# Routing's end in a top-2 mixture of experts: padding rows stored earlier by two queues, the tile table in wide operations, two weights before the first rows, 103 tiles for 104

## The chip, the cores and the metric

The kernel runs on one core of one Trainium2 chip. The metric is the device time of one execution in microseconds (us). Its engines are TensorE (PE, with weight loads shown as PEld), VectorE (DVE), ScalarE (ACT), GpSimd (POOL) and SyncE (SP). A q behind an engine's name (SPq, ACTq, POOLq) is its instruction queue, which also issues DMA transfers. L12 is line 12 of the kernel.

## What is computed

The reference, cut to its frame:

```python
h = tok_ref(...)                       # a state-space kernel, 8 x 256 tokens
h = concatenate([h, txt], axis=1)      # 8 x 768 tokens of width 256
h = h + attn_ref(layernorm(h))         # 16 heads, 4 key/value heads
h = h + ffn_ref(layernorm(h))

def ffn_ref(x, Wr, br, W1, b1, W2, b2):          # E = 8 experts, H = 256
    logits = xf @ Wr + br                        # 6144 tokens
    topk_w, topk_idx = top_k(logits, 2)
    topk_w = softmax(topk_w)
    gate = sum(one_hot(topk_idx, E) * topk_w[..., None], axis=1)
    h = relu(einsum('th,ehf->etf', xf, W1) + b1) # f = 512
    y = einsum('etf,efh->eth', h, W2) + b2
    return einsum('te,eth->th', gate, y)
```

All arithmetic is float32. The kernel computes an expert only for the tokens that chose it.

## The kernel before

There are three stages: the state-space kernel, attention, and a last stage that has routing and the experts in one block, so that each engine's program runs from the one into the other without a barrier. Both belong to the change.

**Routing** (`route`) goes over 8 batches of 768 tokens, six tiles of 128 rows each. TensorE projects attention's output (L983), VectorE adds the residual into `h1` and normalizes into `xn` (L1106), TensorE transposes (L991) and computes the logits (L999), and VectorE picks the two best experts (`choose`) and the slot of every chosen row (`place`). Slots lie in DRAM in `xs_d`, with one region of `STRIDE` = 6144 + 128 rows for each expert; `run` holds the next free slot of every region. GpSimd scatters the rows of a tile to the slots, in 12 indirect DMAs a batch (L966). A batch's turn, logits and placing run beside the next batch's projection; those of the last batch stand in `drain` and have nothing beside them.

Behind the last batch come three steps. First, VectorE computes the tables of the expert tiles (`tile_table`): for each of `NT` = 104 tiles the expert (`exp_i`), the first row in `xs_d` (`src_i`) and the value that gates compare with (`held_by`), by a chain of small operations on 128x8 and 128x1, and then a loop over seven experts of three operations on 128x104. Its first instruction also copies `run` into `tail_i`, the slot behind the last row of each region; its last one raises `table_ready`. Secondly, ScalarE's queue, which waits for `table_ready` in its `drain`, stores 128 padding rows (`pads`) at each of the eight tails (L1068, L1069), so that a tile that is partly filled reads rows which add nothing. Thirdly, SyncE's queue, which waits for `table_ready` at the end of its part of `route`, issues the loads of the first four tiles' weights W1 (L1265, L1266), waits until pads, `h1` and scattered rows have landed (`landed`, L1271), and then loads the rows of the first four tiles (L1261, L1262).

**Experts** (`experts`) runs over the `NT` tiles of 128 rows with a ring of four buffers. For tile j TensorE transposes the rows of tile j+1 (L1293), multiplies tile j by W1 in 16 matmuls (`up`, L1303), and tile j-1 by W2 in 8 (`down`, L1310). ScalarE copies the transposed rows and applies the relu (L1333, L1341). VectorE adds the biases and multiplies by the gate (L1374 to L1394). GpSimd adds the 128 rows of the result into DRAM by an indirect DMA (L1360), for even tiles into the output and for odd ones into `acc2_d`. SyncE loads rows and W1 of tile j+4 as soon as the buffers of tile j are free. Four tiles are written out, a hardware loop runs the middle, and four more are written out (`loop`). At the end GpSimd waits for the adds of both accumulators and adds `acc2_d` into the output in eight DMAs (L1367).

Rows fill at most 96 + 7 tiles, since 12288 rows are 96 x 128 and each of the eight regions rounds up. A tile behind the last filled one repeats it with a gate of zero.

Of the kernel before, what the change touches and what calls it, by code (L numbers as in the profile page):

```python
# [17 lines left out]
P = 128  # L18
NB, SEQ, D = 8, 768, 256
# [4 lines left out]
TT = SEQ // P  # L24
IT = IMG // P
KC = D // P
TOK = NB * SEQ
# [4 lines left out]
NIT = NB * KV  # L32
STRIDE = TOK + P
SLOTS = NE * STRIDE
NT = TOK * TOPK // P + NE
DX = D + 8

F32 = mybir.dt.float32
# [832 lines left out]
def route(nc, block, sb, PS, sem, io, ident, img_d, oT_d, xs_d, acc_d, oT, oT_in, wo_in, h1, run, base, exp_i, src_i, tail_i, held_by, wo, wr, br, weights, weights_in, table_ready):  # L871
# [32 lines left out]
    rstd_ready, run_ready, xn_free = sem("r_rstd_ready"), sem("r_run_ready"), sem("r_xn_free")  # L904
    tr_done, xT_ready, lg_done = sem("r_tr_done"), sem("r_xT_ready"), sem("r_lg_done")
    mask_ready, count_done, gap_ready, ex_ready, idx_ready = (sem(f"r_{n}") for n in ("mask_ready", "count_done", "gap_ready", "ex_ready", "idx_ready"))
    table_dve, zeroed = sem("r_table_dve"), sem("r_zeroed")
    h_stored = sem("r_h_stored")
    norm_dve, pick_dve, place_dve = sem("r_norm_dve"), sem("r_pick_dve"), sem("r_place_dve")
    scattered = [sem(f"r_scattered{q}") for q in range(2)]  # L910
    TURN_AT, LOGITS_AT, COUNTS_AT = 1, 2, 3
# [14 lines left out]
    @block.sync  # L926
    def _(sp):
        sp.nop().then_inc(oT_free, 3)

        assert NE == NB  # L930
        for b in range(NB):
            if b + 1 < NB:
                sp.wait_ge(oT_free, b * TT + 3)
                load_rows(sp, oT, oT_d, oT_in, b + 1, (b + 1) % 2)
            sp.dma_start(b1[:, b], io["b1"][b].rearrange("(c p) -> p c", p=P), allow_slow_non_contiguous=True).then_inc(weights_in, 16)
            sp.dma_start(w2[:, b], io["W2"][b].rearrange("(c p) f -> p c f", p=P)).then_inc(weights_in, 16)
            sp.dma_start(b2[:, b], io["b2"][b].unsqueeze(0).to_broadcast([P, D])).then_inc(weights_in, 16)
        sp.wait_ge(weights_in, 3 * NE * 16)
        sp.wait_ge(table_ready, 1)

    @block.gpsimd
# [86 lines left out]
    @block.scalar  # L1028
    def _(act):
        def root(b):  # L1030
            act.wait_ge(var_ready, b + 1)
            act.activation(sd[:], ve[:], ACT.Sqrt).then_inc(sd_ready, 1)

        def turned(b):
            for n in range(3):
                act.wait_ge(tr_done, b * 3 + n + 1)
                act.activation(xT[:].rearrange("p c s -> p (c s)")[:, 512 * n:512 * n + 512], XT[:, n], ACT.Copy).then_inc(xT_ready, 1)

        def exp_gap(b):
            act.wait_ge(gap_ready, b + 1)  # L1040
            act.activation(ex[:], dl[:], ACT.Exp).then_inc(ex_ready, 1)

        def store(b):
            act.wait_ge(h1_ready, b * TT + (TT + 3))
            act.dma_start(acc_d[bass.ds(b * SEQ, SEQ), :].rearrange("(t p) d -> p t d", p=P), h1[:, b]).then_inc(h_stored, 16)

        def load(b, q):
            act.dma_start(h1[:, b, 0:IT, :], img_d[b].rearrange("(t p) d -> p t d", p=P)).then_inc(h_in[q], 16)
            act.dma_start(h1[:, b, IT:TT, :], io["txt"][b].rearrange("(t p) d -> p t d", p=P)).then_inc(h_in[q], 16)

        def iteration(b, q):
            if not first(b):
                turned(b - 1)
                if not isinstance(b, int):
                    load(b + 1, 1 - q)
                exp_gap(b - 1)
            root(b)
            store(b)

        load(0, 0)  # L1060
        load(1, 1)

        def drain():
            turned(NB - 1)
            exp_gap(NB - 1)
            act.wait_ge(table_ready, 1)
            for x in range(NE):
                row = act.value_load(tail_i[0:1, x:x + 1], min_val=x * STRIDE, max_val=x * STRIDE + TOK)  # L1068
                act.dma_start(xs_d[bass.ds(row, P), :], pads[:]).then_inc(zeroed, 16)  # L1069

        loop(iteration, drain, act)

    @block.vector
    def _(v):
# [88 lines left out]
        def drain():  # L1163
            choose(NB - 1)
            place(NB - 1, 1)
            tile_table(v, sb, table_dve, run, base, tile_no, exp_i, src_i, tail_i, held_by).then_inc(table_ready, 1)

        v.nop().then_inc(h1_ready, 3)
        v.nop().then_inc(mask_ready, 1)
# [3 lines left out]
        v.wait_ge(run_ready, 1)  # L1173
        loop(iteration, drain, v)

    return [(zeroed, 16 * NE), (h_stored, 16 * NB)] + [(scattered[q], NB // 2 * TT * TOPK * 16) for q in range(2)]


def tile_table(v, sb, dve, run, base, j, exp_i, src_i, tail_i, held_by):

    n, cnt, end = sb("t_n", [P, NE]), sb("t_cnt", [P, NE]), sb("t_end", [P, NE])
    ni = sb("t_ni", [P, NE], I32)
    last = sb("t_last", [P, 1])
    jr, e, start, ind = (sb(f"t_{x}", [P, NT]) for x in ("jr", "e", "start", "ind"))
    k = Tally(v, dve)
    link, mark = k.link, k.mark  # L1190
    mark(v.tensor_copy(tail_i[:], run[:]))
    mark(v.memset(e[:], 0.0))
    mark(v.memset(start[:], 0.0))
    link(v.tensor_tensor(n[:], run[:], base[:], ALU.subtract))
    link(v.tensor_scalar(ni[:], n[:], float(P - 1), None, ALU.add))
    link(v.tensor_scalar(ni[:], ni[:], 7, None, ALU.arith_shift_right))
    link(v.tensor_copy(cnt[:], ni[:]))
    link(v.tensor_copy(end[:, 0:1], cnt[:, 0:1]))
    for x in range(1, NE):
        link(v.tensor_tensor(end[:, x:x + 1], end[:, x - 1:x], cnt[:, x:x + 1], ALU.add))  # L1200
    link(v.tensor_scalar(last[:], end[:, NE - 1:NE], -1.0, None, ALU.add))
    link(v.tensor_scalar(jr[:], j[:], last[:], None, ALU.min))
    for x in range(NE - 1):
        link(v.tensor_scalar(ind[:], jr[:], end[:, x:x + 1], None, ALU.is_ge))  # L1204
        mark(v.tensor_tensor(e[:], e[:], ind[:], ALU.add))  # L1205
        link(v.scalar_tensor_tensor(out=start[:], in0=ind[:], scalar=cnt[:, x:x + 1], in1=start[:], op0=ALU.mult, op1=ALU.add))
    link(v.tensor_tensor(start[:], jr[:], start[:], ALU.subtract))
    link(v.tensor_scalar(start[:], start[:], float(P), None, ALU.mult))
    mark(v.tensor_copy(exp_i[:], e[:]))
    link(v.tensor_scalar(ind[:], j[:], last[:], None, ALU.is_gt))  # L1210
    mark(v.scalar_tensor_tensor(out=held_by[:], in0=ind[:], scalar=-2.0 * NE, in1=e[:], op0=ALU.mult, op1=ALU.add))
    return v.scalar_tensor_tensor(out=src_i[:], in0=e[:], scalar=float(STRIDE), in1=start[:], op0=ALU.mult, op1=ALU.add)


def experts(nc, block, sb, PS, sem, io, ident, xs_d, acc_d, acc2_d, exp_i, src_i, held_by, weights, landed, table_ready):
# [26 lines left out]
    def loop(eng, tile):  # L1242

        for n in range(RING):
            tile(n, n)
        with eng.Fori(1, NT // RING - 1) as k:
            for n in range(RING):
                tile(k * RING + n, n)
        for n in range(RING):
            tile(NT - RING + n, n)  # L1250

    def more(j, ahead):
        return not (isinstance(j, int) and j + ahead >= NT)
# [4 lines left out]
    @block.sync  # L1258
    def _(sp):
        def load(j, n):  # L1260
            row = sp.value_load(at(src_i, j), min_val=0, max_val=SLOTS - P)  # L1261
            sp.dma_start(x[:, n, :], xs_d[bass.ds(row, P), :]).then_inc(x_in[n], 16)  # L1262

        def load_w1(j, n):
            ex = sp.value_load(at(exp_i, j), min_val=0, max_val=NE - 1)  # L1265
            sp.dma_start(w1[:, n], io["W1"][bass.ds(ex, 1)].rearrange("o (c p) f -> p (o c) f", p=P)).then_inc(w1_in[n], 16)  # L1266

        for n in range(RING):
            load_w1(n, n)
        for s, value in landed:  # L1270
            sp.wait_ge(s, value)  # L1271
        for n in range(RING):
            load(n, n)

        def tile(j, n):
            if more(j, RING):
                hold(sp, xt_done, j + 1)
                hold(sp, gate_ready, j + 1)
                load(j + RING, n)
                hold(sp, h_done, j + 1)  # L1280
                load_w1(j + RING, n)

        loop(sp, tile)
        sp.wait_ge(summed, 16 * NB)

    @block.tensor
    def _(pe):
# [35 lines left out]

        turn_x(0, 0)
        loop(pe, tile)
        down(NT - 1, 1, expert(NT - 1))

    @block.scalar
    def _(act):
# [23 lines left out]
    @block.gpsimd  # L1353
    def _(pool):
        def tile(j, n):
            hold(pool, y_ready, j + 1)
            q = n % 2
            if not (isinstance(j, int) and j < 2):
                hold(pool, added[q], (j >> 1) * 16)
            pool.indirect_dma_start(out=(acc_d, acc2_d)[q], out_offset=bass.IndirectOffsetOnAxis(ap=row_i[:, n:n + 1], axis=0),  # L1360
                                    in_=y[:, n, :], in_offset=None, compute_op=ALU.add, bounds_check=TOK - 1, oob_is_err=False).then_inc(added[q], 16)

        loop(pool, tile)
        for q in range(2):
            hold(pool, added[q], NT // 2 * 16)
        for b in range(NB):
            pool.dma_start(rows(acc_d, b), rows(acc2_d, b), accum_op=ALU.add, max_dma_last_dim=6144).then_inc(summed, 16)  # L1367

    @block.vector
    def _(v):  # L1370
# [30 lines left out]

        hold(v, table_ready, 1)
        loop(v, tile)
        bias_y(NT - 1, RING - 1)


def program(nc, x, txt, log_dt, inv_A_real, A_imag, B_ri, Wq, Wk, Wv, Wo, Wr, br, W1, b1, W2, b2, rotary, out):
# [71 lines left out]
```

## Time and profile before

| | us |
|---|---|
| three timed runs | 2299.02, 2300.50, 2302.64 (median 2300.5) |
| profiled execution, its own time | 2301.42 |
| profiled execution, its span | 2299.6 |
| the last batch's logits matmuls end | 1831.2 |
| first transpose of an expert tile starts | 1864.9 |
| the last 16 W2 matmuls, of two tiles, start | 2252.2 |
| last adding of the accumulators is issued | 2262.3 to 2269.1, and the span ends at 2299.6 |

The span is what the profiler covers; the execution's own time is 1.8 us more. Times below count from the span's start. PE is busy for 89% of the span, VectorE for 77%.

### The profile page before, as it was taken

The numbers are of one execution on the slowest core, as the hardware profiler recorded it, in microseconds if no ns is written. First come the engines' busy times: TensorE is split into PE (matmuls) and PEld (weight loads), VectorE is DVE, ScalarE is ACT, GpSimd is POOL, SyncE is SP. The second block draws the span as 40 slices with busy tenths as digits, with TensorE's granted clock in tenths as the row PEclk, the third lists the DMA queues.
The fourth block names the chain that finished last, engine by engine and source line by source line (L and its number), as shares of the span: only waits on it lengthen the run. The fifth ranks groups of instructions, "written<-read, shape, count | busy, mean of one in ns | idle before, by whom it ended". The sixth has DMA issues, their size and how long they took to land. (4 is left out here: it accounts for less than half of the span.)

```text
span 2299.6 us, 58897 instructions
## 1 busy us (share of the span) xinstructions
PE 2049.8 (89%) x21124; PEld 1240.5 (54%) x21125; DVE 1771.1 (77%) x3235; ACT 1074.2 (47%) x2468; POOL 890.8 (39%) x849
## 2 busy tenths in 40 slices
PE   0369999999999999999999999986999759999992
PEld 0234444444444444444444444433888659999992
DVE  8769999999999999999999999995344534444441
ACT  2035555655655565656655655653111124434440
POOL 1024444454264354443542642311144434444442
PEclk9889999999999999999999999998999879999996
DMA  5244444543634644444445335434787368888986
GB/s 160 52 104 101 124 110 114 144 111 95 156 105 101 154 104 118 127 117 131 116 104 139 106 98 142 122 84 145 227 283 270 112 186 212 206 215 210 214 209 125
DMA packets 192403, 330.56 MB, mean 144 GB/s; under 512 B 49029, under 2 KB 127680, under 8 KB 192192
## 3 DMA queue, kind: packets, MB, share of 16 engines
q1 hardware_dynamic: 156480, 275.51, 44.3%
q0 software_dynamic: 21888, 38.48, 8.4%
q10 hardware_dynamic: 13824, 13.67, 1.7%
q8 instruction: 143, 2.34, 0.4%
q14 instruction: 68, 0.56, 0.1%
HBM read 221.71 MB, written 105.02 MB: 142 GB/s over the span
## 5 line engine op out<-in xcount | busy, mean ns | idle before, releaser
L733 ACT ACTIVATE a_prob<-ps_s,a_nmax 128x768 f32<-128x768 f32 x768 | 686.3, 898 | 578.5 <-DVE a_nmax L820 578.5
L820 DVE TENSOR_REDUCE a_nmax<-ps_s 128x1 f32<-128x768 f32 x768 | 694.0, 943 | 48.9 <-PE ps_s L664 43.7
L826 DVE STREAM_TRANSPOSE a_probT<-a_prob 128x768 f32<-128x768 f32 x768 | 699.9, 949 | 1.6 <-PE ps_o L671 1.6
L664 PE MATMUL ps_s<-a_kT,a_qT 64*128 64x384 f32 x3072 | 613.8, 513 | 55.2 <-ACT a_prob L733 51.1
L671 PE MATMUL ps_o<-a_probT,a_vrep 32*64 32x384 f32 x12288 | 561.1, 491 | 6.9 <-DVE a_probT L826 5.0
L664 PEld LDWEIGHTS ps_s<-a_kT,a_qT 64*128 64x128 f32 x3072 | 259.3, 186 | 391.5 <-ACT a_prob L733 274.9
L796 POOL TENSOR_TENSOR a_o<-a_o,a_invrow 128x1536 f32<-128x1536 f32 x32 | 110.0, 3438 | 790.8 <-ACT a_o L741 790.8
L671 PEld LDWEIGHTS ps_o<-a_probT,a_vrep 32*64 32x64 f32 x12288 | 243.6, 132 | 293.8 <-issue 130.0
L478 POOL TENSOR_TENSOR a_prod<-a_raw,a_table 128x384 f32<-128x384 f32 x304 | 294.4, 1003 | 28.9 <-DVE a_qp L483 21.8
L1303 PE MATMUL ps_r<-e_xT,e_w 128*128 128x128 f32 x1664 | 204.1, 276 | 0.0
L1310 PE MATMUL ps_r<-ew,e_hT 128*128 x832 | 196.6, 379 | 0.0
L1303 PEld LDWEIGHTS ps_r<-e_xT,e_w 128*128 128x128 f32 x1664 | 195.5, 193 | 0.1
L1341 ACT ACTIVATE e_hT<-ps_r,e_b_now 128x128 f32<-128x128 f32 x416 | 118.9, 368 | 158.7 <-PE ps_r L1303 104.4
L983 PE MATMUL ps_r<-wo,r_oT 128*128 128x256 f32 x768 | 180.9, 397 | 9.6 <-POOL base L949 9.6
L650 PE MATMUL ps_o<-a_xT,wq 128*128 128x384 f32 x512 | 185.8, 501 | 0.0
L983 PEld LDWEIGHTS ps_r<-wo,r_oT 128*128 128x128 f32 x768 | 151.4, 200 | 32.2 <-POOL base L949 10.3
L1310 PEld LDWEIGHTS ps_r<-ew,e_hT 128*128 128x128 f32 x832 | 150.2, 190 | 16.1
L733 ACT ACTIVATION_READ_ACCUMULATOR a_prob<-ps_s,a_nmax 128x1 f32 x768 | 151.0, 197 | 0.0
L966 POOL DMA_INDIRECT xs_d<-r_xn,r_idx x96 | 92.4, 963 | 150.8 <-DVE h L1081 119.8
L650 PEld LDWEIGHTS ps_o<-a_xT,wq 128*128 128x128 f32 x512 | 91.0, 189 | 88.9 <-issue 25.6
L1360 POOL DMA_INDIRECT out_dram<-e_y,e_row_i x52 | 80.7, 1553 | 129.7 <-DVE e_y L1382 126.9
L1360 POOL DMA_INDIRECT acc_d<-e_y,e_row_i x52 | 80.7, 1552 | 115.3 <-DVE e_y L1382 103.3
(211 smaller groups left out, 1348.1 us busy)
## 6 DMA issues: line engine op xcount, KB each, us to landing
e_w<-in_L_ffn_W_dram SPq DMA_DIRECT2D x104, 512.0 KB, 4.3
a_qT<-q_d SPq DMA_DIRECT2D x124, 384.0 KB, 9.1
a_vrep<-v_d SPq DMA_DIRECT2D x128, 192.0 KB, 3.9
a_invrow<-inv_d SPq DMA_DIRECT2D x64, 384.0 KB, 5.2
oT_d<-a_o SPq DMA_DIRECT2D x32, 768.0 KB, 3.2
r_oT<-oT_d SPq DMA_DIRECT2D x64, 384.0 KB, 8.4
q_d<-a_qp SPq DMA_DIRECT2D x31, 768.0 KB, 3.9
e_x<-xs_d SPq DMA_DIRECT2D x104, 132.0 KB, 3.2
```

Of the source, the lines that this page charges most:

```text
L478: eng.tensor_tensor(scratch[n], a, f, ALU.mult).then_inc(done, 1)
L650: last = pe.matmul(X[:, 0:HALF], w, xn[:, k, HALF * c:HALF * c + HALF], start=(k == 0), stop=(k == KC - 1))
L664: last = pe.matmul(S[:, s % 2, r, 0:HALF], qT[rows, par, 2 * hp + c, P * t:P * t + P], kT[rows, par, :], start=True, stop=True)
L671: last = pe.matmul(O[DH * c:DH * c + DH, q, 0:HALF], vrep[rows, j % NQ, j // NQ, :], keys(par, c, j, rows), start=(j == 0), stop=(j == NJ ...
L733: act.activation(prob[:, s % RING, :].rearrange("p (r k) -> p r k", r=2), S[:, s % 2, :, 0:HALF], ACT.Exp, bias=nmax[:, s % RING:s % RING ...
L820: v.tensor_reduce(nmax[:, s % RING:s % RING + 1], S[:, s % 2, :, 0:HALF], AX.XY, ALU.max, negate=True).then_inc(max_ready, 1)
L826: v.transpose(turned(par, s), prob[:, s % RING, :]).then_inc(t_ready, 1)
L983: last = pe.matmul(A[:, t % 3, 0:D], oT[:, q, c // 2, c % 2, P * t:P * t + P], wo[:, c, :], start=(c == 0), stop=(c == KV * 2 - 1))
L1303: last = pe.matmul(H[:, q, P * f:P * f + P], w1[:, n, c, P * f:P * f + P], xT[:, q, P * c:P * c + P], start=(c == 0), stop=(c == KC - 1))
L1310: last = pe.matmul(Y[:, q, 0:D], hT[:, q, P * c:P * c + P], w2[:, bass.ds(ex, 1), c, :], start=(c == 0), stop=(c == FC - 1))
L1341: last = act.activation(hT[:, q, P * f:P * f + P], H[:, q, P * f:P * f + P], ACT.Relu, bias=b1_now[:, n, f:f + 1], scale=1.0)
L1360: pool.indirect_dma_start(out=(acc_d, acc2_d)[q], out_offset=bass.IndirectOffsetOnAxis(ap=row_i[:, n:n + 1], axis=0), in_=y[:, n, :], in_o ...
```

## The change

Pads are stored once `run` is final. VectorE copies `run` into `tail_i` ahead of the table and raises a semaphore of its own, `tail_ready`; ScalarE's queue stores the pads of the odd experts and SyncE's queue those of the even ones, ahead of its wait for `table_ready`. The table's loop over seven experts becomes four operations on 128 x (103 x 7) elements. SyncE loads the weights of two tiles ahead of the wait for the rows, then the rows of four tiles, then the weights of the two others. `NT` is 103; loops and final waits follow.

```diff
-NT = TOK * TOPK // P + NE
+NT = TOK * TOPK // P + NE - 1
...
         sp.wait_ge(weights_in, 3 * NE * 16)
+        sp.wait_ge(tail_ready, 1)
+        for x in range(0, NE, 2):
+            row = sp.value_load(tail_i[0:1, x:x + 1], min_val=x * STRIDE, max_val=x * STRIDE + TOK)
+            sp.dma_start(xs_d[bass.ds(row, P), :], pads[:]).then_inc(zeroed[0], 16)
         sp.wait_ge(table_ready, 1)
...
-            act.wait_ge(table_ready, 1)
-            for x in range(NE):
+            act.wait_ge(tail_ready, 1)
+            for x in range(1, NE, 2):
                 row = act.value_load(tail_i[0:1, x:x + 1], ...)
-                act.dma_start(xs_d[bass.ds(row, P), :], pads[:]).then_inc(zeroed, 16)
+                act.dma_start(xs_d[bass.ds(row, P), :], pads[:]).then_inc(zeroed[1], 16)
...
             place(NB - 1, 1)
-            tile_table(v, sb, table_dve, run, base, tile_no, exp_i, src_i, tail_i, held_by).then_inc(table_ready, 1)
+            v.tensor_copy(tail_i[:], run[:]).then_inc(tail_ready, 1)
+            tile_table(v, sb, table_dve, run, base, tile_no, exp_i, src_i, held_by).then_inc(table_ready, 1)
...
-    mark(v.tensor_copy(tail_i[:], run[:]))
-    mark(v.memset(e[:], 0.0))
-    mark(v.memset(start[:], 0.0))
...
-    for x in range(NE - 1):
-        link(v.tensor_scalar(ind[:], jr[:], end[:, x:x + 1], None, ALU.is_ge))
-        mark(v.tensor_tensor(e[:], e[:], ind[:], ALU.add))
-        link(v.scalar_tensor_tensor(out=start[:], in0=ind[:], scalar=cnt[:, x:x + 1], in1=start[:], op0=ALU.mult, op1=ALU.add))
+    shape = [P, NT, NE - 1]
+    link(v.tensor_tensor(past[:], jr[:].unsqueeze(2).to_broadcast(shape), end[:, 0:NE - 1].unsqueeze(1).to_broadcast(shape), ALU.is_ge))
+    mark(v.tensor_reduce(e[:], past[:], AX.X, ALU.add))
+    link(v.tensor_tensor(skipped[:], past[:], cnt[:, 0:NE - 1].unsqueeze(1).to_broadcast(shape), ALU.mult))
+    link(v.tensor_reduce(start[:], skipped[:], AX.X, ALU.add))
...
-        with eng.Fori(1, NT // RING - 1) as k:
+        whole = (NT - RING) // RING
+        with eng.Fori(1, whole) as k:
...
-        for n in range(RING):
-            tile(NT - RING + n, n)
+        for j in range(whole * RING, NT):
+            tile(j, j % RING)
...
-        for n in range(RING):
+        for n in range(2):
             load_w1(n, n)
         for s, value in landed:
             sp.wait_ge(s, value)
         for n in range(RING):
             load(n, n)
+        for n in range(2, RING):
+            load_w1(n, n)
...
-            hold(pool, added[q], NT // 2 * 16)
+            hold(pool, added[q], (NT + 1 - q) // 2 * 16)
```

The hardware loop's bounds are 1 and 24 where they were 1 and 25 (the upper one excluded), so it runs 23 times four tiles for 24 times, and seven tiles are written out behind it where there were four.

## Rows read from the trace of the kernel before

**Rows 1.** The chain of waits in order of time: start us, length us, what.

```profile
1858.81 3.19 DMA xs_d<-r_pads
1866.65 3.02 PE ps_r L1303 x16
1869.90 1.79 PE ps_r L1303 x16
1873.63 1.79 PE ps_r L1303 x16
...
2247.05 1.79 PE ps_r L1303 x16
...
2258.02 3.69 DMA acc_d<-e_y,e_row_i
2262.29 5.12 POOL out_dram L1367 x6
```

**Rows 2.** The timeline of all engines, 1837 to 1865: start us, length us, engine, line.

```profile
1837.41 0.16 DVE L1191 CAST tail_i<-run 128x8 int32<-128x8 f32 x1
1837.54 0.14 DVE L1192 MEMSET t_e<- 128x104 f32 x1
1837.72 0.10 DVE L1194 TENSOR_TENSOR t_n<-run,base 128x8 f32<-128x8 f32 x1
1838.28 0.95 POOL L966 DMA_INDIRECT xs_d<-r_xn,r_idx  x1 [9.41 <-DVE r_idx L1152]
1840.56 0.27 DVE L1204 TENSOR_SCALAR t_ind<-t_jr,t_end 128x104 f32<-128x104 f32 x1
1846.69 0.27 DVE L1207 TENSOR_TENSOR t_start<-t_jr,t_start 128x104 f32<-128x104 f32 x1
1847.86 0.26 DVE L1212 SCALAR_TENSOR_TENSOR src_i<-t_e,t_start 128x104 int32<-128x104 f32 x1
1849.04 10.11 ACTq L1069 DMA_DIRECT2D xs_d<-r_pads  x8
1849.61 5.39 SPq L1266 DMA_DIRECT2D e_w<-in_L_ffn_W_dram  x4
1852.19 0.96 POOL L966 DMA_INDIRECT xs_d<-r_xn,r_idx  x1 [0.30 <-issue]
1862.73 5.24 SPq L1262 DMA_DIRECT2D e_x<-xs_d  x5
1864.91 0.69 PE L1293 MATMUL ps_r<-ident,e_x 128*128 128x128 f32 x2 [29.89 <-DMA e_x<-xs_d]
```

**Rows 3.** Waits of SyncE's queue, 1800 to 1875: us in total, times, longest.

```profile
SPq L1261 <- DMA xs_d<-r_pads: 4.4, 1, 4.4
SPq L1271 <- DMA xs_d<-r_xn,r_idx: 2.5, 1, 2.5
```

**Rows 4.** DMA issues in 1848 to 1849.3 and 1852 to 1853.3; all W1 loads' landing.

```profile
xs_d<-r_xn,r_idx POOLq DMA_INDIRECT x2, 2.5
xs_d<-r_xn,r_idx POOLq DMA_INDIRECT x1, 5.4
DMA to landing us min/median/max: 3.4/4.3/6.3
```

**Rows 5.** Windows: length, busy us (count) of PE, PEld, DVE, ACT, POOL; clock; DMA share; GB/s.

```profile
1858.00:1860.00 2.00, 0.00 (x0) 0.00 (x0) 0.00 (x0) 0.00 (x0) 0.00 (x0) 0.50 1.06 392
1868.00:1870.00 2.00, 2.00 (x15) 2.00 (x15) 0.00 (x0) 0.22 (x1) 0.00 (x0) 0.72 0.32 85
1900.00:2000.00 100.00, 100.00 (x698) 93.18 (x698) 41.50 (x189) 41.05 (x135) 41.66 (x27) 1.00 0.90 209
```

**Rows 6.** VectorE by line and shape: busy us, mean ns; idle before, releaser.

```profile
L820 DVE TENSOR_REDUCE a_nmax<-ps_s 128x1 f32<-128x768 f32 x768 | 694.0, 943 | 48.9 <-PE ps_s L664 43.7
L295 DVE TENSOR_TENSOR tm<-bare,ct 128x1024 f32<-128x1024 f32 x4 | 4.9, 1224 | 0.1
L258 DVE TENSOR_TENSOR tm<-wre 128x512 f32<-128x512 f32 x2 | 1.4, 693 | 0.0
```

More of the change, by code:

```diff
@@ L906, in route @@
     mask_ready, count_done, gap_ready, ex_ready, idx_ready = (sem(f"r_{n}") for n in ("mask_ready", "count_done", "gap_ready", "ex_ready", "idx_ready"))
-    table_dve, zeroed = sem("r_table_dve"), sem("r_zeroed")
-    h_stored = sem("r_h_stored")
+    table_dve, zeroed = sem("r_table_dve"), [sem(f"r_zeroed{q}") for q in range(2)]
+    h_stored, tail_ready = sem("r_h_stored"), sem("r_tail_ready")
     norm_dve, pick_dve, place_dve = sem("r_norm_dve"), sem("r_pick_dve"), sem("r_place_dve")
@@ L1174, in _, with tile_table @@
         loop(iteration, drain, v)
-    return [(zeroed, 16 * NE), (h_stored, 16 * NB)] + [(scattered[q], NB // 2 * TT * TOPK * 16) for q in range(2)]
-def tile_table(v, sb, dve, run, base, j, exp_i, src_i, tail_i, held_by):
+    return [(zeroed[q], 16 * (NE // 2)) for q in range(2)] + [(h_stored, 16 * NB)] + [(scattered[q], NB // 2 * TT * TOPK * 16) for q in range(2)]
+def tile_table(v, sb, dve, run, base, j, exp_i, src_i, held_by):
     n, cnt, end = sb("t_n", [P, NE]), sb("t_cnt", [P, NE]), sb("t_end", [P, NE])
@@ L1188, in tile_table @@
     jr, e, start, ind = (sb(f"t_{x}", [P, NT]) for x in ("jr", "e", "start", "ind"))
+    past, skipped = (sb(f"t_{x}", [P, NT, NE - 1]) for x in ("past", "skipped"))
     k = Tally(v, dve)
     link, mark = k.link, k.mark
-    mark(v.tensor_copy(tail_i[:], run[:]))
-    mark(v.memset(e[:], 0.0))
-    mark(v.memset(start[:], 0.0))
     link(v.tensor_tensor(n[:], run[:], base[:], ALU.subtract))
@@ L1325, in _ @@
         loop(pe, tile)
-        down(NT - 1, 1, expert(NT - 1))
+        down(NT - 1, (NT - 1) % 2, expert(NT - 1))
     @block.scalar
@@ L1403, in _ @@
         loop(v, tile)
-        bias_y(NT - 1, RING - 1)
+        bias_y(NT - 1, (NT - 1) % RING)
 def program(nc, x, txt, log_dt, inv_A_real, A_imag, B_ri, Wq, Wk, Wv, Wo, Wr, br, W1, b1, W2, b2, rotary, out):
```

## The prediction

> **What bounds the kernel now.** I read the chain of waits first, because the change touches two stretches only and the chain says whether either is on the path. From 1866 to 2254 it is nothing but TensorE: the W1 matmuls of tile 1 start at 1869.90 and those of tile 102 at 2247.05 [rows 1]. That is 377.15 us for 101 tiles, 3.734 us each. The windows confirm it: in 1900 to 2000 TensorE is busy for 100.00 of 100 us at granted clock 1.00, with the DMA engines at 0.90 and every other engine under half [rows 5]. So a tile costs TensorE's time and nothing else, but the DMA engines are close behind.
>
> Ahead of the tiles the chain goes through a wait: pads landing (3.19 us from 1858.81, so at 1862.00), then the first rows (issued at 1862.73), then the first transpose at 1864.91 [rows 1, 2]. The timeline shows what came before, all in series: VectorE's table runs from 1837.41 to 1848.12; ScalarE's queue issues its first pads 0.92 us later (1849.04) and the eighth at 1858.8, one per (10.11 - 0.35) / 7 = 1.39 us; SyncE issues four W1 loads from 1849.61, one per (5.39 - 0.38) / 3 = 1.67 us; GpSimd issues the last batch's 12 scatters from 1838.28 to 1852.19, one per 1.264 us [rows 2].
>
> The waits of SyncE's queue say which came last, and what is next. It waited 2.5 us for scattered rows and after that 4.4 us for pads [rows 3]. The pads ended at 1862.0, hence scattered rows at 1862.0 - 4.4 = 1857.6. That is 5.4 us behind the last scatter's issue (1852.19), where the scatters issued at 1848.39 needed 2.5 [rows 2, 4]. In between the DMA engines turned full: at 1858 to 1860 their share is 1.06 at 392 GB/s [rows 5], with four W1 loads of 512 KB and eight pads of 132 KB. So part of the scatters' lateness is traffic that SyncE put there itself.
>
> **The change part by part.** *Pads from `tail_i` alone.* `tail_i` is written at 1837.41 and done by 1837.57 [rows 2]. Each queue needs the same 0.92 us from release to first issue, so both start at 1838.5, and with four pads at 1.39 us the last goes out at 1838.5 + 3 x 1.39 = 1842.7. Landing takes 3.19 us (the last of before), so they are there at 1845.9. Pads leave the path: 16.1 us earlier than now. Next late are the scattered rows. What SyncE puts behind its four pads is the wait for the table and everything after it; it is done at 1843.0, before the table, so this costs nothing. With a pad at 2 us instead of 1.39 it would be 1844.9, still before the table.
>
> *The scatters.* GpSimd's cadence does not depend on anything that moves: last issue 1852.19. Its landing does. SyncE now puts two W1 loads in front instead of four: 1.05 MB instead of 2.1, started earlier because the table is shorter (below), at 1845.45 + 1.49 = 1846.9 and 1848.6. At the 392 GB/s of the full engines both, with two scatters of 0.14 MB between them, take (1.05 + 0.27) / 0.39 = 3.4 us; counted from about 1.5 us behind the first issue (1848.4) they are through at 1851.8. The last scatter issues after that, so I take the quiet 2.4 to 2.5 us: landed at 1854.6. The bound from the other side is the 5.4 us of now: 1857.6.
>
> *Rows first, weights 2 and 3 later.* From release to the first row load 0.73 us, from its issue to the first transpose 2.18 [rows 2]: 1854.6 + 0.73 + 2.18 = 1857.5, against 1864.91. **Gain 7.4 us** (4.4 at the other bound). The price is that W1 of tile 2 is issued behind four row loads of (5.24 - 0.34) / 4 = 1.22 us each and its own 1.67: 1855.3 + 3 x 1.22 + 1.5 = 1860.5. It lands after 4.3 us in the median (3.4 to 6.3 [rows 4]): 1864.8, with 1866.8 at worst. Tile 2's W1 matmuls want it at 1873.63 - 7.4 = 1866.2 [rows 1]. So 1.4 us are spare in the median and 0.6 are lost at worst. Tile 3 has 3.7 us more to go and its load comes 1.7 later, so it is safer. The loads of tile 4 fall behind by about 1.7 us and are needed some 8 us later: no cost.
>
> *The table.* Seven rounds of three operations go from 1840.56 to 1846.69, 6.13 us [rows 2]. In their place stand two TENSOR_TENSORs and two TENSOR_REDUCEs over 103 x 7 = 721 elements. TENSOR_TENSOR takes 693 ns for 512 and 1224 for 1024 elements [rows 6], thus 1.04 ns an element and 0.91 us for 721. TENSOR_REDUCE over 768 is 943 ns (from PSUM, the only long one), in proportion 0.89 for 721. The sum is 3.6 us and some 0.05 us of linking. That saves 2.5 us; two memsets save 1837.72 - 1837.54 = 0.18. The table is ready at 1848.12 - 2.67 = 1845.45. On the path this is worth nothing, for the scatters end 9 us later, and the first weights need only 5. The bounds are 0 and, if the wide operations cost twice as much, still 0 apart from W1 coming 3.6 us later into the last scatters, which is the 3.0 us of the other bound above.
>
> *103 tiles.* One period less: **3.73 us**. Nothing hides it, for TensorE is the only thing on the chain there. The tail behind the last tile stays: its add lands after 3.69 us and the final adding starts at 2262.29 [rows 1]. That the last tile is now an even one, and that seven tiles are written out for four, I put at 0: the written-out tile 102 starts at 2247.05, in the cadence of the loop. Bounds are -0.5 and +0.5, from the 0.58 us between 2258.02 + 3.69 = 2261.71 and 2262.29.
>
> *TensorE's clock.* It stands at 0.50 (the level of 1.2 GHz) in the pause and is on average at 0.72 in 1868 to 1870 [rows 5], 3 to 5 us behind the first transpose. The pause shortens from 33.7 us (from 1831.2) to 26, and the clock rises in the same way after it. I put this at 0; were the clock full from the start, tile 0's 3.02 us would be 1.79 [rows 1], 1.2 us better.
>
> **Sum.** Span 2299.6 - 7.4 - 3.7 = 2288.5, and the profiled execution's own time is 1.8 more, 2290.3. The median of the runs before is 0.9 under that execution (2300.5 against 2301.42), so I expect a median of **2289.4 us**, 0.48% faster. From here "same" is within 0.2%, 4.6 us, about what a measurement can tell.
>
> A rule that speaks against this: the twelve scatters were issued evenly, 1.264 us apart, although 128x104 operations ran on VectorE beside them [rows 2]; the new operations are three times as long. The Trainium skill (SBUF — State Buffer, Who interferes with whom) says that a VectorE instruction with two inputs in SBUF contends with a GpSimd instruction that reads SBUF, and that the loser of the shared ports waits for the whole instruction. By that rule the two wide TENSOR_TENSORs could each hold a scatter up; this is rival 2.
>
> **The rivals.**
>
> 1. *The scatters still land late* (chance 0.14). Two W1 loads and eight pads are enough to keep the engines full when the last scatters go out. For it: 5.4 us in the crowd of now. Against: by my sum W1 is through at 1851.8. Then 4.4 + 3.7 = 8.1 us are gained: 2292.4.
>
> 2. *The wide operations hold GpSimd up* (0.07). Each of the two 0.91 us TENSOR_TENSORs delays a scatter by up to its length; the row after the scatters shifts by up to 1.8: gain 11.1 - 1.8, 2291.2. Against it is the even cadence beside the short ones.
>
> 3. *Weights of tile 2 late* (0.07). If W1 of tile 2 takes 6.3 us or more because four row loads and W1 of tile 3 lie beside it, TensorE waits 0.6 to 2 us: 2290 to 2291.4.
>
> 4. *The pause was not the pads'* (0.05). If something that the change leaves alone held the first rows, the 7.4 us stay where they are and only the tile goes: 2300.5 - 3.7 = 2296.8, "same". Against it is that the chain and SyncE's waits name the same two releases.
>
> 5. *Slower: the DMA engines set the tile's period* (0.03). The tiles start with two weights in flight instead of four, and the engines are at 0.90 of the period, 3.36 of 3.73 us [rows 5]. If from tile 2 on TensorE waits for W1 in each tile because a lead once lost costs more traffic than the engines can make good, the loss is per tile. It decides from 11.1 / 101 = 0.11 us a tile: the DMA work would have to be 3.84 us for 3.36, and at 3.9 the time is 2289.4 + 101 x 0.17 = 2306.6. Against it: the work per tile does not change, and 0.37 us of each period is free to catch up.
>
> The forecast itself has 0.64. **Range:** its own is 2288 to 2291; rivals 1 to 3 reach up to 2292.4. Below, the clock's 1.2 us, a landing of 2.0 us and the spread of runs (2299.0 to 2302.6) give 2286.5; above, rival 1 with that spread gives 2294. Chances: faster 0.92 (all but rivals 4 and 5), same 0.05, slower 0.03.
>
> **What the profile after would show.** Pads issued from 1838.5 by both queues, four each, landed by 1846. `src_i` ready near 1845.4, with four operations of 0.9 us. The last scatter issued at 1852.2 (if later, rival 2) and SyncE's last wait before the rows ending at 1854.6 (at 1857.6, rival 1), with no wait for pads. The first transpose at 1857.5. No TensorE wait at tile 2 (else rival 3). A period of 3.73 us (more: rival 5). The last W2 row 11 us earlier and the tail of 2262 to 2300 in the same shape. I am wrong in the large if the first transpose still comes after 1861, or if TensorE has idle time between tiles.

## The result, and the profile after

The changed kernel takes 2290.93 us (median of 6 runs, 2288.36 to 2293.79) against 2300.62 (6 runs, 2299.02 to 2302.69): a ratio of 0.9955 with a 95% interval of 0.9943 to 0.9966. The forecast was 2289.4, within 2286.5 to 2294. The profiled execution took 2291.74 us with a span of 2290.0, 9.6 us less than before.

First the chain of waits, in order of time (start us, length us, what). Against [rows 1], the wait for pads is gone, and in its place scattered rows land:

```profile
1853.86 2.43 DMA xs_d<-r_xn,r_idx
1858.23 2.04 DMA e_x<-xs_d
1861.00 2.77 PE ps_r L1310 x16
1864.00 1.79 PE ps_r L1310 x16
...
2237.41 1.79 PE ps_r L1310 x16
...
2242.71 1.74 PE ps_r L1317 x8
2248.40 3.67 DMA out_dram<-e_y,e_row_i
2252.70 5.14 POOL out_dram L1374 x6
```

Then the timeline of the pause, whose counterpart is [rows 2] (`past` and `skipped` are the new wide tiles; L970 is the scatter, L1300 the first transpose):

```profile
1838.00 0.17 DVE L1170 CAST tail_i<-run 128x8 int32<-128x8 f32 x1
1838.88 0.96 POOL L970 DMA_INDIRECT xs_d<-r_xn,r_idx  x1 [9.41 <-DVE r_idx L1156]
1839.09 3.75 ACTq L1073 DMA_DIRECT2D xs_d<-r_pads  x4
1839.24 4.21 SPq L942 DMA_DIRECT2D xs_d<-r_pads  x4
1841.15 0.91 DVE L1207 TENSOR_TENSOR t_past<-t_jr,t_end 128x721 f32<-128x721 f32 x1
1841.41 1.49 POOL L970 DMA_INDIRECT xs_d<-r_xn,r_idx  x1 [0.30 <-issue]
1842.09 0.90 DVE L1208 TENSOR_REDUCE t_e<-t_past 128x103 f32<-128x721 f32 x1
1842.91 0.90 DVE L1209 TENSOR_TENSOR t_skipped<-t_past,t_cnt 128x721 f32<-128x721 f32 x1
1843.20 1.45 POOL L970 DMA_INDIRECT xs_d<-r_xn,r_idx  x1 [0.30 <-issue]
1843.85 0.90 DVE L1210 TENSOR_REDUCE t_start<-t_skipped 128x103 f32<-128x721 f32 x1
1846.15 0.26 DVE L1216 SCALAR_TENSOR_TENSOR src_i<-t_e,t_start 128x103 int32<-128x103 f32 x1
1846.22 1.01 POOL L970 DMA_INDIRECT xs_d<-r_xn,r_idx  x1 [0.30 <-issue]
1847.35 1.74 SPq L1271 DMA_DIRECT2D e_w<-in_L_ffn_W_dram  x2
1853.86 0.96 POOL L970 DMA_INDIRECT xs_d<-r_xn,r_idx  x1 [0.30 <-issue]
1857.11 3.67 SPq L1267 DMA_DIRECT2D e_x<-xs_d  x4
1859.29 0.69 PE L1300 MATMUL ps_r<-ident,e_x 128*128 128x128 f32 x2 [23.67 <-DMA e_x<-xs_d]
1861.54 1.59 SPq L1271 DMA_DIRECT2D e_w<-in_L_ffn_W_dram  x2
```

The reader is to see two things. Pads leave in 1839 to 1843 from both queues and nobody waits for them. And two of the scatters take 1.49 and 1.45 us, each of them beside a wide TENSOR_TENSOR, and a third takes 1.01 beside the last operation of the table; before, all twelve took 0.95 to 0.97.

The pause up to the first transpose is best measured from the first of the last batch's scatters, because that first scatter itself lies anywhere between 1835.2 and 1841.8 us in thirteen traces whose code ahead of it is the same. In that measure the first transpose comes after 1859.29 - 1838.88 = 20.41 us, and came after 1864.91 - 1838.28 = 26.63. The difference in span then has these terms:

| term | before | after | difference |
|---|---|---|---|
| start to first scatter (same code) | 1838.28 | 1838.88 | +0.60 |
| first scatter to first transpose | 26.63 | 20.41 | -6.22 |
| first transpose to W1 of tile 1 | 4.99 | 4.71 | -0.28 |
| W1 of tile 1 to the last W2 | 382.45 | 378.71 | -3.74 |
| last W2 to the end | 47.25 | 47.29 | +0.04 |
| sum | 2299.6 | 2290.0 | -9.6 |

### The profile page after: what moved, and what is told of

Read it like the earlier page. It is cut to its first block and busy times, and to the rows that moved or that the text cites. A ratio compares the mean times of both kernels' runs of the same rounds, so it can differ in the third digit from the quotient of the medians.

```text
span 2290.0 us, 58700 instructions
## 1 busy us (share of the span) xinstructions
PE 2047.1 (89%) x21098; PEld 1237.8 (54%) x21099; DVE 1767.3 (77%) x3209; ACT 1072.8 (47%) x2463; POOL 890.6 (39%) x848
## 5 line engine op out<-in xcount | busy, mean ns | idle before, releaser
L970 POOL DMA_INDIRECT xs_d<-r_xn,r_idx x96 | 93.5, 974 | 150.9 <-DVE h L1085 119.9
```

## The experiments

Each ran in the same way, with the kernel before on the same chip. In the table all times are in us, from one trace of each kernel. "Landed" is the last scatter's landing after its issue, taken where SyncE waited for it last (the first row load is issued 0.82 us behind it). The first transpose and the end of the span count from the first scatter; "clock full" is the time from the first transpose until the granted clock reads 1.00.

| kernel | first to last scatter | landed | first transpose | clock full | end of the span |
|---|---|---|---|---|---|
| before | 13.91 | 5.4, then pads | 26.63 | 4.2 | 461.3 |
| changed | 14.98 | 2.43 | 20.41 | 3.7 | 451.1 |
| changed, second run | 14.98 | 2.42 | 20.38 | 3.5 | 450.9 |
| pads alone | 13.91 | 4.75 | 21.94 | 5.0 | 457.0 |
| table alone | 15.01 | then pads | 24.59 | 6.3 | 460.2 |
| weights' order alone | 13.94 | then pads | 26.02 | 4.5 | 460.9 |
| 103 tiles alone | 13.93 | then pads | 28.42 | 5.3 | 460.1 |
| changed, four weights ahead | 15.01 | 5.05 | 23.03 | 4.4 | 454.1 |
| changed, more products | 15.57 | 2.9 | 21.37 | 6.0 | 453.3 |
| changed, more reduces | 14.95 | 3.24 | 21.10 | 6.4 | 453.2 |
| changed, narrow table | 13.92 | 3.8 | 20.70 | 6.6 | 452.9 |
| changed, table in PSUM | 13.91 | 2.44 | 19.35 | 4.5 | 450.5 |
| the same, second run | 13.89 | 2.42 | 19.31 | 4.6 | 450.5 |

What the fourth column shows is easily missed. TensorE runs at the lower of its two clock levels (0.50, 1.2 GHz) until the full clock is granted, and that comes 3.5 to 6.6 us behind the first transpose, not always at the same distance. What a late clock costs is not in the pause, and only the last column has it.

**Which part brings the pause down?** Four kernels have one part of the change each.

Pads alone (the diff's lines on `tail_ready`, `zeroed` and `pads`, the rest as before):

> The kernel before with one part of the change: pads stored from the counts alone, four by each queue. Old narrow table, four weights ahead of the rows, 104 tiles. Theory A (VectorE's wide operations held two scatters up by 0.5 us each, through the ports that VectorE and GpSimd share): here all 12 scatters last 0.96 us and go out every 1.26 us; the four W1 loads still crowd the last scatters, so these land about 5 us behind their issue; first transpose 4.4 to 6 us earlier than before against the last scatter's issue, time 2294 to 2296 us. Rival B (the pads' traffic, which fills the DMA engines while those two scatters are prepared, made them long): two scatters of 1.4 to 1.5 us here too, last issue 1.0 us late.

Measured: twelve scatters of 0.96 us, the first transpose at 21.94, 4.69 us earlier; ratio 0.997 (0.996 to 0.998). The engines were as full as in the changed kernel when those scatters were prepared (287 GB/s on average in the six microseconds with pads; the DMA engines were busy for 0.94 of the time beside the third scatter and beside the fourth, for 0.93 and 0.99 there), and no scatter was longer. Rival B falls. The chain shows the scatters landing late instead, behind four weights:

```profile
1849.07 4.75 DMA xs_d<-r_xn,r_idx
```

Table alone:

```diff
-    for x in range(NE - 1): (three narrow operations)
+    (two TENSOR_TENSORs and two TENSOR_REDUCEs over 128 x (NT x 7))
```

> The kernel before with the wide table alone; pads still wait for the table. Theory A: two scatters of 1.45 to 1.5 us, last issue 1.0 us later behind the first than the 13.91 us of before, while no pads are in flight. Rival B: all at 0.96 us, 13.91 us. Either way the pads start 2.7 us earlier and end the pause 2.7 us earlier: time 2297.8 us.

Measured: the lengthened scatters are there, with no pads in flight. The timeline's rows:

```profile
1842.10 1.49 POOL L966 DMA_INDIRECT xs_d<-r_xn,r_idx  x1 [0.30 <-issue]
1843.89 1.47 POOL L966 DMA_INDIRECT xs_d<-r_xn,r_idx  x1 [0.30 <-issue]
1854.58 0.96 POOL L966 DMA_INDIRECT xs_d<-r_xn,r_idx  x1 [0.30 <-issue]
```

The pause shrinks by 2.04 us, for pads still hang on the table; ratio 0.9988 (0.9978 to 0.9997). Expected were 2.7. The eight pads took 10.95 us to be issued for 10.11 before, and the last landed after 2.55 us for 3.19.

Order of weights alone:

```diff
-        for n in range(RING):
+        for n in range(2):
             load_w1(n, n)
...
+        for n in range(2, RING):
+            load_w1(n, n)
```

> The kernel before with two weights instead of four ahead of the wait. Pads are still issued until 1858.8 us by ScalarE's queue, so they end the pause. Their last one lands in 2.2 us instead of 3.2 with the weights' traffic gone: 1.0 us earlier, time 2299.5 us, within the noise. Rival: the scatters' landing was what mattered, 4 us or more.

Measured: 0.61 us less pause, for 1.0 expected. The last pads landed after 1.75 us for 3.19, but were issued 0.88 us later. SyncE's queue shows that rows were not what it waited for in the end:

```profile
SPq L1261 <- DMA xs_d<-r_pads: 5.7, 1, 5.7
SPq L1271 <- DMA xs_d<-r_xn,r_idx: 0.5, 1, 0.5
```

The ratio of 0.9985 (0.9976 to 0.9995) is 3.5 us, more than the trace accounts for; with single traces starting up to 6.7 us apart, I don't read more into it. The four ratios of this group rest on the same timings of the kernel before, so an error in those would be in all four. Together they make 0.70% for the 0.45% of the whole change, where the traces make about 7 us (the last column) for 10. Why the timings and the traces differ in this is not known.

103 tiles alone (`NT`, the loop's bounds and the last waits):

> The kernel before with 103 tiles alone. From the first transpose to the last W2 row 3.73 us less, everything else in place: time 2296.8 us. Rival: a tile that only repeats another costs less, or the written-out tail of seven tiles costs something: less than 3 us gained.

Measured: from W1 of tile 1 (1871.93) to the last W2 (2250.81) 378.88 us against 2252.35 - 1869.73 = 382.62, so 3.74 less, as forecast; a repeated tile costs as much as any, and the written-out tail costs nothing. Ratio 0.9987 (0.9977 to 0.9997). But its pause was 1.79 us longer than before, although nothing in the stretch up to the first transpose is changed except 103 elements for 104 in the table: the last pads were issued 0.75 us later against the first scatter and landed after 4.28 us for 3.19. Here SyncE's first W1 load was issued 3.46 us behind the end of the table (1851.37 against 1847.91) for 1.49 before. So where pads end the pause, two traces of almost the same code lie 1.79 us apart, and 0.61 and 2.04 us above are to be read with that. Where scatters end it, two pairs of traces of the same kernel agree within 0.04 us.

**What is the order of weights worth once pads are gone?**

```diff
-        for n in range(2):
+        for n in range(RING):
             load_w1(n, n)
...
-        for n in range(2, RING):
-            load_w1(n, n)
```

> The changed kernel with all four W1 loads ahead of the rows again. Theory: 2.1 MB from 1847.4 us on keep the DMA engines full until after the last scatter is issued; it lands in 4 us or more instead of 2.4 and the first transpose comes 21.5 to 22.5 us behind the first of the 12 scatters (20.4 in the changed kernel, 26.6 before): 1 to 2 us slower. Rival: the earlier table and pads have cleared the way, the landing stays 2.4 us and the order of weights is worth nothing.

Measured: 23.03, 2.62 us later than the changed kernel, by the landing of the last scatter (5.05 for 2.43 us). The same edit was worth 0.61 us while pads ended the pause. The expected direction, somewhat more than expected. The ratio of 0.9965 (0.9949 to 0.998) has an interval that overlaps that of the changed kernel, so the loss is shown by the trace alone.

**What lengthens the scatters?** The product is repeated in one kernel, the reduce in the other. The first edit adds three products to the one that stands ahead of it, so there are four, and not the three that the expectation names:

```diff
+    for n in range(3):
+        link(v.tensor_tensor(skipped[:], past[:], cnt[...].to_broadcast(shape), ALU.mult))
```

> The changed kernel with the wide product (TENSOR_TENSOR, two inputs in SBUF) done three times in place of once; the result is the same. Theory A (each such operation holds a scatter that starts beside it until its end): two more scatters of 1.4 to 1.5 us, so 15.9 to 16.8 us from the first to the last scatter for 15.0; first transpose as much later. Rival C (any long VectorE operation, a reduce too, holds GpSimd): the same here, and as much in the kernel with more reduces.

```diff
-    link(v.tensor_reduce(start[:], skipped[:], AX.X, ALU.add))
+    for n in range(4):
+        link(v.tensor_reduce(start[:], skipped[:], AX.X, ALU.add))
```

> The changed kernel with the last wide TENSOR_REDUCE (one input) done four times in place of once; the result is the same. Theory A: still two long scatters and 15.0 us from the first to the last. Rival C: four or five long scatters, 16.4 us. The table is ready 2.8 us later in both.

The timeline of the kernel with more products:

```profile
1843.56 0.90 DVE L1209 TENSOR_TENSOR t_skipped<-t_past,t_cnt 128x721 f32<-128x721 f32 x1
1843.84 1.46 POOL L970 DMA_INDIRECT xs_d<-r_xn,r_idx  x1 [0.30 <-issue]
1844.49 2.81 DVE L1211 TENSOR_TENSOR t_skipped<-t_past,t_cnt 128x721 f32<-128x721 f32 x3
1845.60 1.59 POOL L970 DMA_INDIRECT xs_d<-r_xn,r_idx  x1 [0.30 <-issue]
1847.49 0.96 POOL L970 DMA_INDIRECT xs_d<-r_xn,r_idx  x1 [0.30 <-issue]
```

And that of the kernel with four reduces:

```profile
1846.80 3.72 DVE L1211 TENSOR_REDUCE t_start<-t_skipped 128x103 f32<-128x721 f32 x4
1847.91 0.96 POOL L970 DMA_INDIRECT xs_d<-r_xn,r_idx  x1 [0.30 <-issue]
1849.18 0.96 POOL L970 DMA_INDIRECT xs_d<-r_xn,r_idx  x1 [0.30 <-issue]
```

Each long scatter ends 0.84 us behind the end of a TENSOR_TENSOR: 1842.90 behind 1842.06 and 1844.65 behind 1843.81 in the changed kernel. The three products that were added, 2.81 us in a row, lengthened one more scatter, by 0.63 us; I had expected two and 15.9 us or more from the first scatter to the last, where 15.57 were measured; the next scatter starts when the products are over. Three more reduces lengthened none: 14.95 us, and the scatter at 1847.91 starts inside one of them. Rival C falls.

The third scatter of 1.01 us fits in: its neighbour, the operation that writes `src_i`, has two inputs in SBUF and only 0.26 us, ends at 1846.41, and the scatter ends at 1847.23, 0.82 behind it. It is 1.01 or 1.02 us in the four traces where that operation runs when a scatter starts (changed in both runs, four weights ahead, table alone), and it is the last 0.05 of the 1.07 us. The times of the kernels with more products and with more reduces (ratios 0.9968, interval 0.9952 to 0.9983, and 0.9957, 0.9944 to 0.997) do not separate them from the changed kernel.

**Can it be taken away?** One operand of each wide TENSOR_TENSOR comes from PSUM, and the product goes there too:

```diff
+    endp, cntp = PS[:, 2, 0:NE - 1], PS[:, 2, 16:16 + NE - 1]
+    skipped = (103 x 7 elements of PS[:, 0:2])
...
+    mark(v.tensor_copy(cntp, cnt[:, 0:NE - 1]))
+    mark(v.tensor_copy(endp, end[:, 0:NE - 1]))
...
-    link(v.tensor_tensor(past[:], jr..., end[:, 0:NE - 1]..., ALU.is_ge))
+    link(v.tensor_tensor(past[:], jr..., endp..., ALU.is_ge))
-    link(v.tensor_tensor(skipped[:], past[:], cnt[:, 0:NE - 1]..., ALU.mult))
+    link(v.tensor_tensor(skipped, past[:], cntp..., ALU.mult))
```

> The changed kernel with one operand of each wide TENSOR_TENSOR in PSUM (the counts and their running sums are copied there, the product goes there), so that none has two inputs in SBUF. Theory A: all 12 scatters 0.96 us, 13.9 us from the first to the last for 15.0, first transpose 19.3 us behind the first scatter for 20.4, time 1.1 us less. Rival C: as the changed kernel, 15.0 us.

Its timeline, first the operation and the scatter beside it, then the last scatter and the first transpose:

```profile
1838.60 0.91 DVE L1211 TENSOR_TENSOR t_past<-t_jr,ps_r 128x721 f32<-128x721 f32 x1
1838.86 0.96 POOL L970 DMA_INDIRECT xs_d<-r_xn,r_idx  x1 [0.30 <-issue]
...
1850.24 0.96 POOL L970 DMA_INDIRECT xs_d<-r_xn,r_idx  x1 [0.31 <-issue]
...
1855.68 0.69 PE L1304 MATMUL ps_r<-ident,e_x 128*128 128x128 f32 x2 [22.62 <-DMA e_x<-xs_d]
```

The operation is as long, at the same place, and the scatter beside it isn't: 13.91 us of scatters, first transpose at 19.35, as theory A had it to 0.05 us. This operation carries the comparison, for the product with its output in PSUM starts 0.23 us behind its scatter, where it started 0.29 ahead of it in the changed kernel. Ratio 0.9952 (0.9935 to 0.9968). It was run again beside the changed kernel and one with the old table:

> The changed kernel unaltered, beside the next two on one chip. First transpose 20.4 us behind the first of the last 12 scatters; 10 us faster than before, as in its first timing.

> The version with one operand of the wide products in PSUM again: 13.9 us of scatters and the first transpose 19.35 us behind the first one, as in its first run. Time 1.1 us under the changed kernel on the same chip, which is less than the spread of single runs (5 us); the rival is that some other stretch takes it back, which the medians of the two would show as no difference or the other sign.

> The changed kernel with the old table of 21 narrow operations. Theory A: 12 scatters of 0.96 us, 13.9 us from the first to the last. The table is ready 2.3 us later against the first scatter than in the changed kernel, so two W1 loads fall beside the last scatters and these land 0 to 2.5 us later: first transpose 19.4 to 21 us behind the first scatter, the same time as the changed kernel within 1 us. Rival: the wide table was a gain for the path, and here the first transpose comes at 22 us or more.

Against 2302.33 us before on that chip: changed 2292.51 (ratio 0.9957, 0.9943 to 0.9971), in PSUM 2290.02 (0.9951, 0.9938 to 0.9965), narrow table 2294.16 (0.9965, 0.9951 to 0.9979). The version in PSUM beats the kernel before beyond doubt. That it beats the changed one is shown for the pause (1.06 and 1.07 us in two pairs of traces) and not for the time: the ratios have the right sign both times, the intervals overlap. The traces show that another stretch takes part of it back: the clock is full 4.5 and 4.6 us behind the first transpose for 3.7 and 3.5, W1 of tile 1 starts 4.99 us behind it for 4.54, and 0.6 and 0.4 us are left at the end of the span. The narrow table gives even scatters, but its weights come 2.3 us later into the last of them, which land after 3.8 us: 0.29 us behind the changed kernel. In the changed kernel the wide table gives with one hand 1.36 us of landing and takes with the other 1.07 us of scatters. But at the end of the span the narrow table is 1.8 us behind (452.9 for 451.1), since its clock is full only 6.6 us behind the first transpose; the medians differ by 1.65. Whether the clock would come as late in another trace of it, one trace can't say.

## Why the prediction was right, point by point

*The sum:* -11.1 us forecast, -9.6 in the pair of traces, -9.7 in the medians. The range held. Of the two numbers on record, 2290.93 us lies nearer to rival 2's 2291.2 than to the forecast's 2289.4. There is luck in how closely the traces fit the medians, since spans of single traces hold starts up to 6.7 us apart; the pause (-6.22 for -7.4) and the tile don't hang on that.

*103 tiles:* forecast 3.73, measured 3.74 in the changed kernel and 3.74 alone. The tail was put at 0: 0.04.

*Pads leave the path:* right. They were issued from 1839.1 and 1839.2 (1838.5 forecast, and 0.6 of that is the later start), 1.13 and 1.29 us apart where I had 1.39 from the crowd of before. Rival 4 (something else held the rows) is refuted by pads alone, 4.69 us.

*The scatters' landing:* forecast 2.4 to 2.5 us with two weights ahead, measured 2.43; with four ahead 5.05 and 4.75. So rival 1 did not come, and its cause was the right one: in both kernels with four weights ahead it was there.

*The scatters' cadence:* this is the step that was wrong. "GpSimd's cadence does not depend on anything that moves: last issue 1852.19" was off by 1.07 us (14.98 for 13.91). Rival 2, to which I gave 0.07, is what happened, at 0.53 and 0.49 us a time where its bound was 0.91, and 0.05 more beside the short operation that writes `src_i`. That is two thirds of the 1.5 us by which the span missed; the later start, 0.60, is the rest, and 0.09 more from release to row load and 0.28 less of warming up nearly cancel. The even cadence beside the 128x104 operations, which I had held against rival 2, was no evidence on longer ones: a scatter ended 0.82 to 0.84 us behind the operation that held it and takes 0.96 by itself, so an operation that is over 0.13 us behind the scatter's start leaves no mark. The Trainium skill (SBUF — State Buffer, Who interferes with whom) had named the condition, two inputs in SBUF against a GpSimd instruction that reads there; the traces agree with it each way that was tried: more such products held one scatter more, more reduces none, and with an operand in PSUM no scatter was held.

*The table:* 3.6 us forecast for the four wide operations, 3.61 measured (0.91 + 0.90 + 0.90 + 0.90). I had it worth nothing on the path. It is worth 1.36 us there, since it clears the weights away from the last scatters, which my own sum of 3.4 us of traffic used without pricing it; net of the cadence 0.29 up to the first transpose, and 1.8 at the end of the span, where the later clock of the narrow table's trace is counted.

*Weights of tiles 2 and 3 behind the rows:* issued from 1861.54, in time; W1 of tile 2 starts at 1867.57 in the cadence of the rest, and rival 3 did not come. Nor did rival 5, whose sign would be a longer period: 378.71 us for 101 of 103 tiles and the last W2 is one period of 3.74 less than before, and TensorE is busy for 100.00 of 100 us again:

```profile
1900.00:2000.00 100.00, 100.00 (x700) 93.19 (x699) 41.06 (x186) 40.74 (x134) 41.43 (x27) 1.00 0.88 212
```

*TensorE's clock:* 0.76 in 1862 to 1864 and 1.00 behind it, that is, full (2.4 GHz) 3.7 us behind the first transpose, where it was 4.2 before. I had put the difference at 0, since the clock would rise "in the same way"; it was 0.28 us of gain. That this was small is luck: over the thirteen traces the clock is full 3.5 to 6.6 us behind the first transpose, and W1 of tile 1 starts 4.54 to 5.51 us behind it (4.82 before, all by the timeline). What decides it was not tried.

## What to carry to other kernels

Edits to a chain of waits don't add up: the order of weights was worth 0.61 us by itself and 2.62 once pads were gone, the table 2.04 by itself and 0.29 beside the other edits, all up to the first transpose, because another wait was last. (That pads, table and order together make 6.22 where the three alone make 7.34 is within the 1.79 us by which a pause that pads end differs between two traces.) So price each edit against the wait that is last once the others are made. Follow the time past the end of the pause, up to where TensorE's clock is full. And when a VectorE operation gets longer beside GpSimd's DMA work, count its inputs in SBUF; short operations that ran there free of charge prove nothing.

## What had not been expected of the hardware

- A wide TENSOR_TENSOR with both inputs in SBUF (0.91 us) holds an indirect DMA that GpSimd starts beside it until it ends: 1.45 to 1.59 us for 0.96. A TENSOR_REDUCE of 0.90 us does not, nor does the same TENSOR_TENSOR with one input in PSUM. In all held scatters the end comes 0.82 to 0.84 us behind the operation's, and all of them start while it runs. That also accounts for the short operations, all but one: in the kernel before, a TENSOR_TENSOR of 0.27 us is over 0.13 us behind the start of the sixth scatter, which takes 0.97; the others with two inputs are over sooner, or start behind a scatter. The exception is the fourth scatter, 0.96 us: a SCALAR_TENSOR_TENSOR (L1206) runs from 0.07 us ahead of its start until 0.30 behind it. That operation took 0.37 us there and 0.32 elsewhere. No kernel tried widths between.
- TensorE's clock stays at 0.50 for 3.5 to 6.6 us behind the first transpose, in thirteen traces with the same work there. Between the traces of the changed kernel and the one with the narrow table that was 1.5 us of the span (1.8 less the 0.29 of the pause).
- From the end of the table to SyncE's first W1 load it takes 0.94 to 0.95 us in all eight traces of the changed kernel and of the versions made from it. It takes 2.11 with pads alone, and where SyncE stood in one long wait up to the table (the kernel before, and table, tiles and weights' order alone) 1.49, 1.26, 3.46 and 3.50. In the three longest, small instructions of SyncE's queue that take 0.02 to 0.2 us elsewhere follow each other in steps of 0.70 us or twice that for some microseconds (with 103 tiles alone from 1849.26 to 1854.87), and in two of them ScalarE's do so too. What the steps are was not tried, nor whether they are there when no profile is taken. That they made the pause of 103 tiles alone longer is likely and not shown: pads took 10.87 us to be issued there, and 10.95 with the table alone, where the first W1 load was not late.
- The value loads of ScalarE's queue between pads took 0.28 to 1.03 us before, beside the weights' traffic, and 0.29 to 0.49 in the changed kernel; pads were 1.39 us apart there and 1.13 here.
